# Attention scores of two query tiles made together, half-height low-key products, loads spread behind transposing DMAs, and half of a share added by VectorE

## The chip, the cores and the metric

One core of a Trainium2 chip (trn2). The time is the device time of one execution in microseconds, from the first to the last work of the core. Engines: PE (TensorE: matmul; PEld is its weight load), DVE (VectorE), ACT (ScalarE), POOL (GpSimd), SP (SyncE, which here only issues DMAs). "Tile" below is a query tile of 128 rows.

## What is computed

The reference is a layer of attention with gating experts, followed by a recurrent layer with its own experts. The change touches the attention alone. There, for 4 batches of 1024 rows of 128 and 16 heads of 64:

```python
scores = jnp.einsum('bhqd,bhkd->bhqk', q, k) * SCALE
kb = -p * jnp.log1p(a * dist)                  # dist = |key position - query position|
attn = jax.nn.softmax(scores + kb[None], axis=-1)
out = jnp.einsum('bhqk,bhkd->bhqd', attn, v)
out = out.transpose(0, 2, 1, 3).reshape(Bb, Ss, H * D)
return out @ out_w.T
```

## The kernel before

`project` makes queries, keys and values and writes each as two bf16 parts, a high one and the low remainder, to DRAM. `attend` then runs over 32 pairs of heads and batches (`it`; head pair `g` outside, batch `b` inside). One `it` has two heads `s` = 0 and 1 of eight query tiles each, so 16 tiles `n`, and 512 in all. For each tile:

- PE (`scores`, L943 to L953) makes 128 x 1024 scores in one of two PSUM buffers `score_ps`. Each half of 512 keys takes two matmuls over 128 rows: the stack of high and low queries by high keys twice (`QS` by `KS`, L951), and by low keys twice (`QS` by `KL`, L952). It waits until the tile two before has been read (`biased`) and, on a head's first tile, for the head's loads (`qk_in`).
- DVE (`bias_max`, L1018 to L1029) adds the bias table `TB` to the scores, writes them to SBUF and takes the maximum: L1028, the custom operation. It signals `biased`.
- ACT (`exp`, L1102) makes the probabilities and their sums, with four buffers `PR`.
- PE (`turn`, L960) transposes the high parts of the probabilities. DVE (L1050, odd tiles) or ACT (L1109, even tiles) copies them to `PT`.
- POOL (`low`, L1134) subtracts the high part and leaves the low one in one of four buffers `LQ`. SP (`lo_turn`, L911) transposes that with a DMA to `LO`. A buffer is free for POOL when its DMA has landed.

For each head of eight tiles there follow: PE (`by_v`) multiplies the transposed high parts by the values in four steps (L979) and the low parts in two steps of column halves (L984), 64 output rows for one half of the tiles beside 64 for the other. DVE and ACT (`take_out`) split the result into bf16 parts (L1055, L1058, L1114). PE (`out`, L997 to L999) multiplies by the head's rows of the output weights, in two PSUM buffers `pv_ps` of four tiles each. DVE (`scale_share`, L1068) scales both by the inverse sums (`SH`), and POOL (`add_share`, L1142) adds each to the accumulator `SACC`.

All engines walk through steps `u` of their own program in order, `n = u + 2` being the tile whose values step is next. In step `u` PE makes the scores of tile `u + 13`, transposes tile `u + 11`, then does the output (`n % 8 == 7`) and one values step (`n % 8 < 6`). DVE does `take_out` (`n % 8 == 6`), then tile `u + 13`, then `invert` (5), `scale_share` (7) and the copy of tile `u + 11`. ACT does its part of `take_out`, then exp of tile `u + 12`, then its copy. POOL subtracts tile `u + 11` and adds shares at `u % 8` of 6 and 7. There is no planner: the order is that of these programs, with semaphores between them.

SP's queue is in order as well. `units` (L913 to L927) issues one `lo_turn` a tile. Behind tile 2 of each head stands `load_v`. Behind tile 8 stand the six loads of the next `it`'s head 0 (`load_scores_in`, L802 to L811, 128 KB each), behind tile 15 those of its head 1. In the last batch of a head pair each is followed by `load_table` (L814 to L817): the bias table of the next pair, 128 rows of 1920 f32, 960 KB.

Of the kernel before, what the change touches and what calls it, by code (L numbers as in the profile page):

```python
# [20 lines left out]
P = 128  # L21
# [598 lines left out]
def project(nc, K, io, sb, ps, sem):  # L620
# [71 lines left out]
    with nc.Block() as block:  # L692

        @block.sync
        def _(sp):
# [16 lines left out]
            for s in range(2):  # L712
                load_scores_in(sp, K, 0, s)
                load_table(sp, K, 0, s)
# [87 lines left out]
def load_scores_in(sp, K, ix, s):  # L802

    q = K.qkscr[bass.ds(ix % B * G + ix // B, 1)].rearrange("o p k c -> (o p) k c")
    rows = slice(s * DH, s * DH + DH)
    sp.dma_start(K.QS[s][0:DH, :], q[rows, 0, :]).then_inc(K.qk_in[s], DMA)
    sp.dma_start(K.QS[s][DH:P, :], q[rows, 1, :]).then_inc(K.qk_in[s], DMA)
    sp.dma_start(K.KS[s][0:DH, :], q[rows, 2, :]).then_inc(K.qk_in[s], DMA)
    sp.dma_start(K.KS[s][DH:P, :], q[rows, 2, :]).then_inc(K.qk_in[s], DMA)
    sp.dma_start(K.KL[s][0:DH, :], q[rows, 3, :]).then_inc(K.qk_in[s], DMA)  # L810
    sp.dma_start(K.KL[s][DH:P, :], q[rows, 3, :]).then_inc(K.qk_in[s], DMA)  # L811


def load_table(sp, K, g, s):  # L814

    tab = bass.AP(tensor=K.fscr.tensor, offset=(g * 2 + s) * FLEN, ap=[[1, P], [1, TAB]])
    sp.dma_start(K.TB[s][:], tab).then_inc(K.tab_in[s], DMA)  # L817


def attend(nc, K, io, sb, ps, sem):  # L820
# [18 lines left out]
    QS, KS, KL, TB = K.QS, K.KS, K.KL, K.TB  # L839
# [12 lines left out]
    SH = [sb(f"share{i}", [P, 4, D]) for i in range(2)]  # L852
# [36 lines left out]
    def at(it, n, add):  # L889

        return it * n + add

    with nc.Block() as block:

        @block.sync
        def _(sp):
# [15 lines left out]

            def units(g, b, last=False):  # L913
                it = g * B + b
                for n in range(U):
# [5 lines left out]
                    if n in (BT, U - 1) and not (last and b == B - 1):  # L921
                        s = n // (U - 1)
                        sp.wait_ge(s_ready, at(it, U, BT * (s + 1)))
                        sp.wait_ge(biased, at(it, U, BT * (s + 1)))
                        load_scores_in(sp, K, it + 1, s)
                        if b == B - 1:
                            load_table(sp, K, g + 1, s)  # L927
# [13 lines left out]
        def _(pe):  # L941
            def scores(it, n):
                s, t, k = n // BT % 2, n % BT, n // U  # L943
                if t == 0:
                    pe.wait_ge(qk_in[s], at(it, 6 * DMA, 6 * DMA * (k + 1)))
                if not (isinstance(it, int) and it == 0 and n < 2):
                    pe.wait_ge(biased, at(it, U, n - 1))
# [748 lines left out]
```

## Time and profile before

| | us |
|---|---|
| median of 3 runs | 2019.54 |
| lowest, highest | 2015.58, 2019.97 |
| the profiled execution, its own time | 2019.78 |
| span of that execution (first to last instruction) | 2018.0 |
| mean granted clock of PE, as a share of 2.4 GHz | 0.956 |

The page begins so. Section 1 is busy time, share of the span and instructions of each engine. Section 2 cuts the span into 40 slices of 50.5 us; a digit is the busy share in tenths, PEclk the clock granted to PE, DMA the mean busy share of 16 DMA engines.

```profile
PE 1810.2 (90%) x12166; PEld 1052.0 (52%) x12356; DVE 1517.4 (75%) x2940; ACT 1149.4 (57%) x1691; POOL 1470.0 (73%) x865
...
PE   3959879999779999999999989999999999599978
...
DVE  8303548999888888878878888878888888698841
ACT  3413533222267777777777767777777777322123
POOL 4260274555579999989989899899899899655521
PEclk8779979999989999999999999999999999799989
DMA  4212483446569888888888888888888888500001
```

The attention is slices 12 to 34: the long stretch in which PE and POOL stand at 9, ACT at 7 and DMA at 8. A busy PE counts matmuls whose ends are modelled, so a 9 there is not proof that PE is the limit.

### The profile page before, as it was taken

What the parts mean: (1) busy time and instruction counts of PE and PEld (TensorE: products, weight loads), DVE (VectorE), ACT (ScalarE), POOL (GpSimd) and SP (SyncE); (2) the same over time, 40 slices, a digit from 0 to 9 for tenths busy, and PEclk for the clock granted to TensorE, in tenths of its full rate; (3) what the DMA queues carried; (4) which work ended last, traced back from release to release, by engine and by line L of the source; (5) the groups of instructions that cost most, each with busy time, mean ns of one, the idle gap of its engine ahead of it and who ended that gap; (6) DMA issues with size and microseconds to landing.
All of it is one profiled execution on the core that took longest, in us unless ns stands there. A gap on an engine that the chain in (4) does not pass through costs nothing. (4 is left out here: it accounts for less than half of the span.)

```text
span 2018.0 us, 39811 instructions
## 1 busy us (share of the span) xinstructions
PE 1810.2 (90%) x12166; PEld 1052.0 (52%) x12356; DVE 1517.4 (75%) x2940; ACT 1149.4 (57%) x1691; POOL 1470.0 (73%) x865
## 2 busy tenths in 40 slices
PE   3959879999779999999999989999999999599978
PEld 2636523333245555555555555555555555356656
DVE  8303548999888888878878888878888888698841
ACT  3413533222267777777777767777777777322123
POOL 4260274555579999989989899899899899655521
PEclk8779979999989999999999999999999999799989
DMA  4212483446569888888888888888888888500001
GB/s 138 94 42 62 127 203 128 151 146 210 167 135 180 185 194 178 193 185 180 193 180 183 186 177 184 188 182 182 187 183 184 197 184 184 135 1 1 1 6 37
DMA packets 714150, 295.28 MB, mean 146 GB/s; under 512 B 619264, under 2 KB 678658, under 8 KB 714064
## 3 DMA queue, kind: packets, MB, share of 16 engines
q1 hardware_dynamic: 678240, 257.81, 56.5%
q10 hardware_dynamic: 33792, 33.56, 4.9%
q0 software_dynamic: 2048, 3.15, 1.2%
q8 instruction: 23, 0.38, 0.1%
q14 instruction: 47, 0.39, 0.1%
HBM read 102.39 MB, written 58.85 MB: 80 GB/s over the span
## 5 line engine op out<-in xcount | busy, mean ns | idle before, releaser
L1134 POOL TENSOR_TENSOR probs_lo<-probs 128x1024 bf16<-128x1024 f32 x512 | 957.1, 1901 | 78.9 <-DMA probs_t_lo<-probs_lo 51.3
L1102 ACT ACTIVATE probs<-scores,neg_max 128x1024 f32<-128x1024 f32 x512 | 588.6, 1150 | 264.0 <-DVE neg_max L1028 232.6
L1028 DVE CUSTOM_DVE_ANT_0 scores<-score_ps,bias_tab 128x1024 f32<-128x1024 f32 x512 | 624.8, 1221 | 116.9 <-issue 111.6
L952 PE MATMUL score_ps<-k_lo_lo,q_hi_lo 128*128 128x512 bf16 x1024 | 392.8, 384 | 35.8 <-DVE ident_bf L1088 15.6
L960 PEld LDWEIGHTS turn_ps<-ident_bf,probs 128*128 128x128 bf16 x4096 | 273.2, 98 | 144.6 <-issue 25.3
L960 PE MATMUL turn_ps<-ident_bf,probs 128*128 128x128 bf16 x4096 | 314.9, 220 | 18.9 <-ACT probs L1102 18.8
L951 PE MATMUL score_ps<-k_hi_hi,q_hi_lo 128*128 128x512 bf16 x834 | 321.4, 385 | 2.1 <-DMA k_lo_lo<-qk_parts 2.1
L979 PE MATMUL pv_ps<-probs_t_hi,v_hi_lo 128*128 128x512 bf16 x1024 | 262.9, 380 | 10.4 <-DVE share L1068 7.0
L1109 ACT COPY probs_t_hi<-turn_ps 128x1024 bf16<-128x1024 bf16 x256 | 255.9, 1000 | 21.2 <-PE turn_ps L960 17.3
L798 PE MATMUL proj_ps<-xn_t,wqk 128*128 128x512 f32 x512 | 231.1, 604 | 7.2 <-DVE rotated L670 5.8
L684 POOL TENSOR_TENSOR qk_parts<-rotated,qk_parts 128x1024 bf16<-128x1024 f32 x64 | 136.3, 2132 | 111.0 <-ACT qk_parts L678 110.8
L951 PEld LDWEIGHTS score_ps<-k_hi_hi,q_hi_lo 128*128 128x128 bf16 x1024 | 100.8, 98 | 168.8 <-DVE neg_max L1028 44.5
L1050 DVE COPY probs_t_hi<-turn_ps 128x1024 bf16<-128x1024 bf16 x256 | 175.6, 686 | 0.0
L1142 POOL TENSOR_TENSOR s<-s,share 128x512 f32 (+1 forms) x128 | 163.7, 1279 | 6.9 <-DVE share L1068 6.9
L798 PEld LDWEIGHTS proj_ps<-xn_t,wqk 128*128 128x128 f32 x512 | 92.1, 189 | 146.3 <-issue 92.3
L678 ACT CAST qk_parts<-rotated 128x1024 bf16<-128x1024 f32 x64 | 66.9, 1046 | 170.6 <-DVE rotated L670 161.7
L952 PEld LDWEIGHTS score_ps<-k_lo_lo,q_hi_lo 128*128 128x128 bf16 x1024 | 101.2, 99 | 92.0 <-issue 3.0
L1350 POOL TENSOR_TENSOR q_state<-state,q_t 128x1024 f32<-128x1024 f32 x32 | 76.5, 2391 | 81.8 <-DVE state L1294 72.5
L984 PE MATMUL pv_ps<-probs_t_lo,v_hi_lo 128*64 128x512 bf16 x1024 | 134.7, 385 | 0.0
L979 PEld LDWEIGHTS pv_ps<-probs_t_hi,v_hi_lo 128*128 128x128 bf16 x1024 | 87.4, 98 | 81.1 <-DVE share L1068 19.5
L1102 ACT ACTIVATION_READ_ACCUMULATOR probs<-scores,neg_max 128x1 f32 x512 | 96.1, 188 | 0.0
L997 PE MATMUL pv_ps<-wo_parts,out_t_hi 128*128 (+1 forms) x512 | 92.7, 224 | 2.8 <-DVE out_t_lo L1058 2.8
(213 smaller groups left out, 2392.6 us busy)
## 6 DMA issues: line engine op xcount, KB each, us to landing
qk_parts<-qk_parts ACTq DMA_DIRECT2D x64, 512.0 KB, 3.2
q_hi_lo<-qk_parts SPq DMA_DIRECT2D x128, 128.0 KB, 2.8
k_hi_hi<-qk_parts SPq DMA_DIRECT2D x128, 128.0 KB, 2.9
k_lo_lo<-qk_parts SPq DMA_DIRECT2D x128, 128.0 KB, 3.0
v_hi_lo<-v_parts SPq DMA_DIRECT2D x64, 256.0 KB, 3.2
bias_tab<-bias_by_distance SPq DMA_DIRECT2D x16, 960.0 KB, 6.2
v_parts<-v_parts SPq DMA_DIRECT2D x24, 512.0 KB
probs_t_lo<-probs_lo SPq DMA_TRANSPOSE x512, 3.3
```

The lines of the kernel that those rows point to most:

```text
L684: g.tensor_tensor(parts[s][:, 1::2, :], rq[s][:], parts[s][:, 0::2, :], ALU.subtract).then_inc(lo_ready, 1)
L798: mm = pe.matmul(pp[s][:, i, :], wqk[r][:, i, :], rows, start=True, stop=True)
L951: pe.matmul(o[:, cs[c]], QS[s][:, q], KS[s][:, cs[c]], start=True, stop=False)
L952: mm = pe.matmul(o[:, cs[c]], QS[s][:, q], KL[s][:, cs[c]], start=False, stop=True)
L960: mm = pe.transpose(tp[n % 2][:, k, :], PRB[n % NP][:, k * P:k * P + P], ident16[:])
L979: mm = pe.matmul(ov[i][:], VV[h][:, k, :], PT[:, r:r + 4, k, :], start=(k == 0), stop=False, skip_group_check=True)
L1028: v.tensor_tensor_reduce(SB[n % 2][:], sp_[n % 2][:], TB[s][:, j:j + S], -1.0, 3.0e38, ALU.add, ALU.min, neg_max[:, n % 16:n % 16 + 1]).th ...
L1050: v.tensor_copy(PT[:, n % U, :, :], tp[n % 2][:]).then_inc(hi_dve, 1)
L1102: act.activation(PR[n % NP][:], SB[n % 2][:], ACT.Exp, bias=neg_max[:, m:m + 1], scale=-1.0, accum_out=row_sum[:, m:m + 1]).then_inc(exped, 1)
L1109: act.copy(PT[:, n % U, :, :], tp[n % 2][:]).then_inc(hi_act, 1)
L1134: g.tensor_tensor(LQ[n % NL][:], PR[n % NP][:], PRB[n % NP], ALU.subtract).then_inc(low_made, 1)
L1142: g.tensor_tensor(acc, acc, SH[c][:], ALU.add).then_inc(added, 1)
```

## The change

- Scores: on even tiles PE makes the scores of tiles `n` and `n + 1` in one go: the high-key products of `n`, then of `n + 1`, then the low-key products of `n` (signal), then of `n + 1` (signal).
- Low-key products: each half of 512 keys is one matmul over 64 rows instead of 128, high queries by low keys; the product of low queries by low keys is left out. The first half of the keys uses rows 0 to 63 (`QS`), the second rows 64 to 127, where a new tile `QX` holds the high queries again. `KL` holds only the half of the keys that its rows need.
- Loads: seven instead of six for each head, of 64 rows; the two of `KL` are 64 KB each, the others 128 KB. They are issued one behind each transposing DMA, behind tiles 6 to 11 for head 0 of the next `it` and 14, 15 and 0 to 3 for head 1, the last two together. The wait for `s_ready` comes ahead of the first. The bias table is loaded in four quarters of 480 columns, behind the last four of these.
- Share: DVE adds the first four tiles of each head into `SACC` itself, scaling and adding in one operation of 128 x 128 for each (four `scalar_tensor_tensor`); POOL adds the other four. One buffer `SH` instead of two.

```diff
@@ -710,8 +710,9 @@
             for s in range(4):
                 sp.wait_ge(qk_wr[s], DMA * NJ // 4 + 1)
             for s in range(2):
-                load_scores_in(sp, K, 0, s)
-                load_table(sp, K, 0, s)
+                load_scores_in(sp, K, 0, s, slice(0, 7))
+                for k in range(4):
+                    load_table(sp, K, 0, s, k)
         @block.gpsimd
         def _(g):
@@ -799,22 +800,26 @@
                         mm.then_inc(qk_ready, 1)
 
-def load_scores_in(sp, K, ix, s):
+def scores_parts(K):
+
+    low, high, every = slice(0, DH), slice(DH, P), slice(0, S)
+    return [(K.QS, low, 0, every), (K.QS, high, 1, every), (K.KS, low, 2, every), (K.KS, high, 2, every),
+            (K.QX, high, 0, every), (K.KL, low, 3, slice(0, CH)), (K.KL, high, 3, slice(CH, S))]
+
+
+def load_scores_in(sp, K, ix, s, parts):
     q = K.qkscr[bass.ds(ix % B * G + ix // B, 1)].rearrange("o p k c -> (o p) k c")
     rows = slice(s * DH, s * DH + DH)
-    sp.dma_start(K.QS[s][0:DH, :], q[rows, 0, :]).then_inc(K.qk_in[s], DMA)
-    sp.dma_start(K.QS[s][DH:P, :], q[rows, 1, :]).then_inc(K.qk_in[s], DMA)
-    sp.dma_start(K.KS[s][0:DH, :], q[rows, 2, :]).then_inc(K.qk_in[s], DMA)
-    sp.dma_start(K.KS[s][DH:P, :], q[rows, 2, :]).then_inc(K.qk_in[s], DMA)
-    sp.dma_start(K.KL[s][0:DH, :], q[rows, 3, :]).then_inc(K.qk_in[s], DMA)
-    sp.dma_start(K.KL[s][DH:P, :], q[rows, 3, :]).then_inc(K.qk_in[s], DMA)
-
-
-def load_table(sp, K, g, s):
-
-    tab = bass.AP(tensor=K.fscr.tensor, offset=(g * 2 + s) * FLEN, ap=[[1, P], [1, TAB]])
-    sp.dma_start(K.TB[s][:], tab).then_inc(K.tab_in[s], DMA)
+    for dst, to, kind, cols in scores_parts(K)[parts]:
+        sp.dma_start(dst[s][to, cols], q[rows, kind, cols]).then_inc(K.qk_in[s], DMA)
+
+
+def load_table(sp, K, g, s, k):
+
+    n = TAB // 4
+    tab = bass.AP(tensor=K.fscr.tensor, offset=(g * 2 + s) * FLEN + k * n, ap=[[1, P], [1, n]])
+    sp.dma_start(K.TB[s][:, k * n:k * n + n], tab).then_inc(K.tab_in[s], DMA)
 
 def attend(nc, K, io, sb, ps, sem):
...
@@ -910,6 +915,21 @@
                 sp.sem_inc(add_begun, 1)
                 sp.dma_start(LO[:, r, :, :], LQ[n % NL][:], transpose=True).then_inc(lo_in[n % NL], DMA)
+            def ahead(g, b, n, last):
+
+                it, s = g * B + b, (0 if 6 <= n < 12 else 1)
+                i = (n - 6) % BT
+                if i >= 6 or (n < 6 and isinstance(it, int) and it == 0) or (n >= 6 and last and b == B - 1):
+                    return
+                ix, due = (it, 0) if n < 6 else (it + 1, BT * (s + 1))
+                if i == 0:
+                    sp.wait_ge(s_ready, at(it, U, due))
+                load_scores_in(sp, K, ix, s, slice(i, i + 1 if i < 5 else 7))
+                if i >= 2 and b == (0 if n < 6 else B - 1):
+                    if i == 2:
+                        sp.wait_ge(biased, at(it, U, due))
+                    load_table(sp, K, g if n < 6 else g + 1, s, i - 2)
+
             def units(g, b, last=False):
                 it = g * B + b
                 for n in range(U):
@@ -918,13 +938,7 @@
                     if n % BT == 2 and not (isinstance(it, int) and it == 0):
                         sp.wait_ge(op_ready, at(it, 4, 2 * (s + 1) - 4))
                         load_v(it, s)
-                    if n in (BT, U - 1) and not (last and b == B - 1):
-                        s = n // (U - 1)
-                        sp.wait_ge(s_ready, at(it, U, BT * (s + 1)))
-                        sp.wait_ge(biased, at(it, U, BT * (s + 1)))
-                        load_scores_in(sp, K, it + 1, s)
-                        if b == B - 1:
-                            load_table(sp, K, g + 1, s)
+                    ahead(g, b, n, last)
             for s in range(2):
                 load_v(0, s)
@@ -940,17 +954,21 @@
         @block.tensor
         def _(pe):
             def scores(it, n):
-                s, t, k = n // BT % 2, n % BT, n // U
-                if t == 0:
-                    pe.wait_ge(qk_in[s], at(it, 6 * DMA, 6 * DMA * (k + 1)))
-                if not (isinstance(it, int) and it == 0 and n < 2):
-                    pe.wait_ge(biased, at(it, U, n - 1))
-                o, q = sp_[n % 2], slice(t * P, t * P + P)
+                s, k = n // BT % 2, n // U
+                if n % BT == 0:
+                    pe.wait_ge(qk_in[s], at(it, 7 * DMA, 7 * DMA * (k + 1)))
                 cs = [slice(c * CH, c * CH + CH) for c in range(2)]
-                for c in range(2):
-                    pe.matmul(o[:, cs[c]], QS[s][:, q], KS[s][:, cs[c]], start=True, stop=False)
-                    mm = pe.matmul(o[:, cs[c]], QS[s][:, q], KL[s][:, cs[c]], start=False, stop=True)
-                mm.then_inc(s_ready, 1)
+                pair = [(i, sp_[i], slice((n + i) % BT * P, (n + i) % BT * P + P)) for i in range(2)]
+                for i, o, q in pair:
+                    if not (isinstance(it, int) and it == 0 and n < 2):
+                        pe.wait_ge(biased, at(it, U, n + i - 1))
+                    for c in range(2):
+                        pe.matmul(o[:, cs[c]], QS[s][:, q], KS[s][:, cs[c]], start=True, stop=False)
+                for i, o, q in pair:
+                    for c in range(2):
+                        rows = slice(c * DH, c * DH + DH)
+                        mm = pe.matmul(o[:, cs[c]], (QS, QX)[c][s][rows, q], KL[s][rows, cs[c]], start=False, stop=True)
+                    mm.then_inc(s_ready, 1)
             def turn(it, n):
                 pe.wait_ge(exped, at(it, U, n + 1))
@@ -1001,7 +1019,7 @@
             def step(it, u, there):
                 n = u + LV
-                if there(u + LS):
+                if there(u + LS) and (u + LS) % 2 == 0:
                     scores(it, u + LS)
                 if there(u + LT):
                     turn(it, u + LT)
...
@@ -1062,11 +1080,18 @@
                 h = hh % 2
                 v.wait_ge(recip, at(it, 2, hh + 1))
-                for c in range(2):
-                    v.wait_ge(op_ready, at(it, 4, 2 * hh + c + 1))
-                    v.wait_ge(added, at(it, 4, 2 * hh + c + 1))
-                    v.tensor_tensor(SH[c][:], ov[c][:], last_axis(inv[:, BT * h + 4 * c:BT * h + 4 * c + 4], D),
-                                    ALU.mult).then_inc(scaled, 1)
+                v.wait_ge(scaled, at(it, 4, 2 * hh + 2))
+                v.wait_ge(op_ready, at(it, 4, 2 * hh + 1))
+                for k in range(4):
+                    row = (it % B) * BT + k
+                    acc = K.SACC[:, row, :] if isinstance(row, int) else K.SACC[:, bass.ds(row, 1), :].rearrange("p o d -> p (o d)")
+                    ins = v.scalar_tensor_tensor(out=acc, in0=ov[0][:, k, :], scalar=inv[:, BT * h + k:BT * h + k + 1],
+                                                 in1=acc, op0=ALU.mult, op1=ALU.add)
+                ins.then_inc(scaled, 1)
+                v.wait_ge(op_ready, at(it, 4, 2 * hh + 2))
+                v.wait_ge(added, at(it, 2, hh + 1))
+                v.tensor_tensor(SH[:], ov[1][:], last_axis(inv[:, BT * h + 4:BT * h + 8], D),
+                                ALU.mult).then_inc(scaled, 1)
             def step(it, u, there):
                 n = u + LV
@@ -1133,23 +1158,22 @@
                     g.wait_ge(lo_in[n % NL], at(it, DMA * U // NL, DMA * (n // NL)))
                 g.tensor_tensor(LQ[n % NL][:], PR[n % NP][:], PRB[n % NP], ALU.subtract).then_inc(low_made, 1)
-            def add_share(it, h, c):
-
-                g.wait_ge(scaled, at(it, 4, 2 * h + c + 3))
+            def add_share(it, h):
+
+                g.wait_ge(scaled, at(it, 4, 2 * h + 4))
                 g.sem_inc(add_begun, 1)
-                row = (it % B) * BT + 4 * c
+                row = (it % B) * BT + 4
                 acc = K.SACC[:, row:row + 4, :] if isinstance(row, int) else K.SACC[:, bass.ds(row, 4), :]
-                g.tensor_tensor(acc, acc, SH[c][:], ALU.add).then_inc(added, 1)
+                g.tensor_tensor(acc, acc, SH[:], ALU.add).then_inc(added, 1)
             def step(it, u, there):
                 if there(u + LT):
                     low(it, u + LT)
-                for c in range(2):
-                    if there(u) and u % BT == BT - 2 + c:
-                        add_share(it, u // BT, c)
+                if there(u) and u % BT == BT - 1:
+                    add_share(it, u // BT)
             g.wait_ge(zeroed, 1)
-            g.nop().then_inc(added, 2)
+            g.nop().then_inc(added, 1)
             run(g, step)
 
...
```

## Rows read from the trace of the kernel before

**Rows 1.** Windows, one head without a table load: busy us of each engine (x instructions).
```profile
core 0: us, PE busy (x) PEld busy (x) DVE busy (x) ACT busy (x) POOL busy (x), PEclk, DMA share, GB/s
1048.30:1065.50 17.20, 16.85 (x145) 9.99 (x148) 14.56 (x33) 13.16 (x20) 17.20 (x11) 1.00 0.84 174
```

**Rows 2.** Timeline of POOL: start, us, engine, line, operation, [idle before <- until what].
```profile
1015.35 11.15 POOL L1134 TENSOR_TENSOR probs_lo<-probs 128x1024 bf16<-128x1024 f32 x6 [5.21 <-DMA probs_t_lo<-probs_lo]
1026.46 1.27 POOL L1142 TENSOR_TENSOR s<-s,share 128x512 f32 x1
1027.69 1.90 POOL L1134 TENSOR_TENSOR probs_lo<-probs 128x1024 bf16<-128x1024 f32 x1
...
1043.74 1.29 POOL L1142 TENSOR_TENSOR s<-s,share 128x512 f32 x1
```

**Rows 3.** Instructions of L1134 and L911, ns min/median/max, first and last start, engine's waits.
```profile
L1134 POOL TENSOR_TENSOR probs_lo<-probs x512: 1887/1897/2875, 561.7 to 1730.1; 128x1024 bf16<-128x1024 f32 x171
  DMA probs_t_lo<-probs_lo: 51.3, 14
...
L911 SPq DMA_TRANSPOSE probs_t_lo<-probs_lo x512: 1230/1240/5216, 563.7 to 1732.1; - x171
```

**Rows 4.** Timeline of SP's queue: a table load; then a head's loads and transposes.
```profile
1006.21 0.42 SPq L817 DMA_DIRECT2D bias_tab<-bias_by_distance  x1
...
1060.90 0.53 SPq L806 DMA_DIRECT2D q_hi_lo<-qk_parts  x1
...
1064.89 2.69 SPq L911 DMA_TRANSPOSE probs_t_lo<-probs_lo  x2
```

**Rows 5.** The page's DMA issues: KB each, median us from issue to landing.
```profile
k_lo_lo<-qk_parts SPq DMA_DIRECT2D x128, 128.0 KB, 3.0
v_hi_lo<-v_parts SPq DMA_DIRECT2D x64, 256.0 KB, 3.2
```

**Rows 6.** Timeline of all engines, parts of two tiles.
```profile
1002.74 0.61 PE L960 MATMUL turn_ps<-ident_bf,probs 128*128 128x128 bf16 x8
...
1003.18 1.03 PE L979 MATMUL pv_ps<-probs_t_hi,v_hi_lo 128*128 128x512 bf16 x4
...
1009.26 0.61 PE L960 MATMUL turn_ps<-ident_bf,probs 128*128 128x128 bf16 x8
...
1009.80 1.05 PE L984 MATMUL pv_ps<-probs_t_lo,v_hi_lo 128*64 128x512 bf16 x8
1010.61 0.08 DVE L1028 DVE_READ_ACCUMULATOR2_ANT neg_max<- 128x1 f32 x1
...
1010.78 0.10 PEld L951 LDWEIGHTS score_ps<-k_hi_hi,q_hi_lo 128*128 128x128 bf16 x1 [0.41 <-DVE neg_max L1028]
...
1011.87 1.22 DVE L1028 CUSTOM_DVE_ANT_0 scores<-score_ps,bias_tab 128x1024 f32<-128x1024 f32 x1 [0.57 <-issue]
```

**Rows 7.** Timeline of DVE at a head's first tiles and at its scaling.
```profile
1200.33 1.22 DVE L1028 CUSTOM_DVE_ANT_0 scores<-score_ps,bias_tab 128x1024 f32<-128x1024 f32 x1 [0.57 <-issue]
...
1203.59 1.22 DVE L1028 CUSTOM_DVE_ANT_0 scores<-score_ps,bias_tab 128x1024 f32<-128x1024 f32 x1
...
1206.49 1.28 DVE L1068 TENSOR_TENSOR share<-pv_ps,inv_sum 128x512 f32<-128x512 f32 x2
```

**Rows 8.** Groups of DVE by shape: count | busy us, mean ns | idle before.
```profile
L250 DVE SCALAR_TENSOR_TENSOR s<-s,ln_moe_rstd,attn_nb_rows 128x128 f32<-128x128 f32 x32 | 8.8, 347 | 0.1
```

**Rows 9.** Timelines of ACT and of POOL, an exp and its subtraction.
```profile
963.02 1.15 ACT L1102 ACTIVATE probs<-scores,neg_max 128x1024 f32<-128x1024 f32 x1 [1.43 <-DVE neg_max L1028]
...
964.17 0.99 ACT L1109 COPY probs_t_hi<-turn_ps 128x1024 bf16<-128x1024 bf16 x1
...
964.34 1.90 POOL L1134 TENSOR_TENSOR probs_lo<-probs 128x1024 bf16<-128x1024 f32 x1 [0.34 <-ACT probs L1102]
```

**Rows 10.** Timeline of PE after a long stop, and the window that follows.
```profile
1167.30 1.03 PE L960 MATMUL turn_ps<-ident_bf,probs 128*128 128x128 bf16 x8 [4.33 <-ACT probs L1102]
...
1166.53:1169.94 3.41, 2.64 (x25) 2.65 (x26) 1.56 (x4) 2.85 (x6) 3.41 (x3) 0.50 1.08 222
```

More of the change, by code:

```diff
@@ L837, in attend @@
     recip = sem("recip")
-    QS, KS, KL, TB = K.QS, K.KS, K.KL, K.TB
+    QS, QX, KS, KL, TB = K.QS, K.QX, K.KS, K.KL, K.TB
     VV = [sb(f"v_hi_lo{s}", [P, BT, 2 * DH], BF16) for s in range(2)]
@@ L851, in attend @@
     OL = [sb(f"out_t_lo{i}", [P, CH], BF16) for i in range(2)]
-    SH = [sb(f"share{i}", [P, 4, D]) for i in range(2)]
+    SH = sb("share", [P, 4, D])
     ot_hi, wo_ready = [sem(f"ot_hi{c}") for c in range(2)], sem("wo_ready")
@@ L1022, in bias_max @@
                 if t == 0:
-                    v.wait_ge(tab_in[s], (it + n // U) // B * DMA + DMA)
+                    v.wait_ge(tab_in[s], (it + n // U) // B * (4 * DMA) + 4 * DMA)
                 if not (isinstance(it, int) and it == 0 and n < 2):
@@ L1615, in program @@
             K.QS = [sb_in(f"q_hi_lo{s}", [P, S], BF16) for s in range(2)]
+            K.QX = [sb_in(f"q_hi_again{s}", [P, S], BF16) for s in range(2)]
             K.KS = [sb_in(f"k_hi_hi{s}", [P, S], BF16) for s in range(2)]
```

## The prediction, made before the changed kernel was built or run

> **What bounds the kernel now.** The windows of the attention stage come first. In a head without a table load [rows 1] POOL is busy for the whole 17.2 us and PE for 16.85; DVE and ACT have slack. A head is eight query tiles, so POOL's timeline [rows 2] is next: eight subtractions (L1134) and two share additions (L1142) repeat every 17.28 us (1026.46 to 1043.74) without idle. The stage, from the first L1134 to the last, is 1730.1 + 1.9 - 561.7 = 1170.3 us [rows 3] for 64 heads: 64 x 17.28 = 1105.9, plus 51.3 in which POOL waited for transposing DMAs [rows 3], plus 13.1 of filling and small waits. One of the waits for DMA is the 5.21 us in [rows 2]; the table load of 960 KB stands just before it in SP's queue (1006.21 in [rows 4]). There are 14 such loads, two in each of seven changes of head pair. The profiled execution took 2019.8 us (the median of the runs is 2019.5), so all else is 2019.8 - 1170.3 = 849.5 us, which the change doesn't touch but for the first loads.
>
> **What the parts save by themselves.** POOL loses one of two additions, 1.23 us (1026.46 to 1027.69 in [rows 2]): 16.05 a head. SP issues eight transposes, six loads and one load of values in a head. Two transposes in a row took 2.69, one issue is 1.24 [rows 3], so they stand 1.45 apart; the six loads before them took 1064.89 - 60.90 = 3.99, or 0.66 each [rows 4]. A load moved behind a transpose costs the same 0.66, for it is an instruction with its own registers wherever it stands. With seven loads and the values SP needs 8 x 1.45 + 8 x 0.66 = 16.9 us, and 4 x 0.6 more in the 14 heads with table quarters. On PE a 128-column transpose passes in 0.056 (eight in 0.45), a 512-column product of L979 in 0.217 (four in 0.87), and a column half of L984 in 0.096, two side by side [rows 6]. Row halves aren't in these rows. I take them to run side by side like the column halves, the nearest row: the four low-key products of a tile pair then take 0.43 where they took 0.87. The other bound is one after another, nothing saved. DVE gives one multiplication of 0.6 (the second of two in [rows 7]) for four of 128x128. The nearest row, L250, has 0.347 each [rows 8]; quarters of 0.6 would be 0.15. I take 0.25 each, 1.0 for four, as they don't wait for one another. If those savings were all, SP would be last with 16.9.
>
> **What the new order adds: the tile pair.** So far the scores of tile n+1 are made while VectorE reads tile n; two PSUM buffers allow it. In the pair, s_ready of the even tile n comes only after the first products of n+1, and these go into the buffer that tile n-1 leaves when it is biased. So when DVE has done n-1, tile n can't be ready. The price of that: DVE ends an L1028 at 1010.61 + 0.08 = 1010.69 and PE's weight load follows at 1010.78, 0.09 later; four matmuls start from 1010.78 on, the last at 1011.43, and L1028 starts at 1011.87, 0.44 later [rows 6]. New: 0.09 + 2 x 0.217 + 0.44 = 0.96, and a change of array shape.
> The column halves price that change: a block of transposes starts 0.44 before L979 (1002.74 to 1003.18) but 0.54 before L984 (1009.26 to 1009.80), and eight halves that need some 0.86 held the array for 0.98 [rows 6]. So 0.1 in and 0.1 out, and the same for row halves, nearest to them in kind: 0.2 a pair on PE, 0.1 in DVE's gap, which becomes 1.06.
> The Trainium skill says in "TensorEngine Tiling (Array Packing)", Key Properties, that changing the tiling mode drains TensorE, which speaks against a pair that changes it twice; the 0.1 above agrees. Without a price for it the period below is 0.3 us shorter, the time 19 us less.
>
> **One head worked through.** Zero is the start of L1028 on the head's first tile, 16. In us:
> - Tile 17's L1028 starts at 3.26, behind the reciprocal and three operations on the output (1200.33 to 1203.59 in [rows 7]), and ends at 4.49.
> - With the gap, tile 18 runs from 5.55 to 6.78. ACT must first copy tile 16's transposes (PE 5.63 to 6.08, copy 6.25 to 7.25 by the 0.99 of [rows 9]), so exp(18) starts at 7.25. POOL starts 1.32 after an exp does (963.02 to 964.34 in [rows 9]): low(18) from 8.55 to 10.4, the share addition to 11.65, low(19) to 13.5.
> - DVE scales after tile 18: op_ready is there at 6.9, four small operations end at 7.95, the multiplication at 8.6; tile 19 from 8.6 to 9.83.
> - PE: first products of 21 at 9.92. A pair with two value steps costs PE 4 x 0.217 + 0.43 + 0.2 + 2 x 0.45 + 2 x 0.87 = 4.13; the pair with a column-half step 4.33. (DVE would need 2 x 1.23 + 1.06 = 3.5.) So first products of 25 start at 18.4, and tile 24's L1028 at 18.4 + 0.43 + 0.1 + 0.44 = 19.4.
> DVE and PE now alternate where they overlapped, and need 19.4 us a head, though neither is busy for more than 17.
> **And the late loads.** All six loads of a half used to follow tile 8 (or 15). Now the last two stand behind the transpose of tile 11 (or 19), and scores(16) (or 24) wait for both. In my head that transpose is issued at 13.55, its loads at 15.0 and 15.65, and the last lands 3.0 later, at 18.65 (k_lo_lo in [rows 5]; 64 KB instead of 128 saves little, since 256 KB take only 3.2). First products of 24 start at 18.75, not at 17.95, and those of 25 at 19.2: tile 24's L1028 at 20.15. So 20.1 a head. A table quarter issued behind them at 16.3 lands by 19.5 (the row of 256 KB) and costs nothing. The moved waits on s_ready and biased cost nothing either: they ask for tiles that PE made well before POOL's subtraction of the tile whose transpose stands in front; transposes are queued behind them, and these are later by their own low part.
> The bursts that held the transposes are gone, and with them the 51.3 us.
>
> **The sum.** 64 x 20.1 = 1286.4, plus 13.1, plus 849.5 is 2149; for the first two heads, whose loads are there, 1 less: 2148 us, 6.4% slower. Bounds: row halves one after another, 0.6 a head more (2186); a landing 0.3 earlier or later, 19 us less or more; small DVE operations of 0.15 or 0.35, nothing as long as the loads come last; no price for the change of shape, 19 less. Together 2110 to 2200.
>
> **Rivals.**
> - The parts save what they save and the rest overlaps: SP's 16.9 is the period. 64 x 16.9 = 1081.6, tables 14 x 2.4 = 33.6, with 13.1 and 849.5 1978, faster by 2.1%. For it: PE gets shorter, and four buffers lie between exp and the transposes. Against: no buffer lies between the two score tiles and DVE, and buffers behind can't help a front that comes late. It decides once a pair's gap on DVE is under 0.5 us.
> - The pair costs less than I sum, and the loads come in time: no price for shapes, small operations cheap, 18.5 a head: 64 x 18.5 + 862.6 = 2047. For it: in my head the loads are late by only 0.75, little for a chain of ten steps.
> - In between, 18.0 to 18.2 a head: no difference, because the 51.3 us pay for the pair.
> - The clock falls. After 4.33 us without a matmul eight transposes took 1.03 instead of 0.61, and the granted clock of the next 3.41 us was 0.50, 1.2 GHz [rows 6, 10]. In my head PE is idle for 2.1 us before tile 19's products and has work for four fifths of the time; no row shows what that does. One such stretch a head costs up to half of 3.41, 1.7 us: 64 x 1.7 = 109, 2257.
>
> **How the numbers follow.** Forecast 0.57; pair alone 0.18; falling clock 0.07; SP's period 0.13; no difference 0.05. The range runs from the no-difference case (2015) to past the forecast's own upper bound (2215), and leaves out SP's period and the falling clock, 0.20. A measurement of this kernel can tell 0.2% (4 us) from no change. Faster by more than that 0.13, within it 0.05, slower by more 0.82.
>
> **What would show it.** In the trace of after: POOL's L1134 waits for ACT every head, and heads are 20 us long; on DVE some 2.3 us from an odd tile's L1028 to the even one's after it, 1.23 inside a pair; PE waits for k_lo_lo at each head's first scores; the low-key products start two at a time; no stop of POOL at the table loads. It would be wrong if POOL or SP had no idle time, or if an even tile's L1028 followed the odd one's without a gap.

## The result, and the profile after

| | us |
|---|---|
| before, median | 2017.56 |
| changed, median of 4 runs | 2190.10 (2184.83 to 2198.07) |
| ratio | 1.0835 (95%: 1.0806 to 1.0863) |
| the profiled execution of the changed kernel | 2198.07, span 2196.3 |
| its mean granted clock | 0.937 of 2.4 GHz |

The changed kernel is 8.35% slower by the ratio on record (the two medians divided give 8.55%, within its interval of 8.06 to 8.63); 6.4% was forecast. "Before" is the same kernel as above, with one more run beside the changed one. Two sections of its page, the busy times and three lines of the 40 slices (54.9 us each):

```profile
PE 1823.5 (83%) x12198; PEld 977.1 (44%) x12356; DVE 1551.2 (71%) x3132; ACT 1148.4 (52%) x1691; POOL 1404.5 (64%) x801
...
PE   3959689998688888888788888788888888779978
...
POOL 4340555555687777777687787777777777654521
PEclk8879789999799999999999999999999999988989
```

In slices 11 to 34 PE has gone from 9 to 8 and POOL from 9 to 7. POOL does less (1470.0 us became 1404.5) in more time: it isn't the limit. The instructions of its subtraction (line 1134 before, 1159 now) say what it waits for:

```profile
L1159 POOL TENSOR_TENSOR probs_lo<-probs x512: 1886/1895/3938, 562.1 to 1902.0; 128x1024 bf16<-128x1024 f32 x171
its engine sat idle before it (us, times) until:
  ACT probs L1127: 311.6, 325
  DMA probs_t_lo<-probs_lo: 2.2, 3
```

Against [rows 3]: the 51.3 us of waits for transposing DMAs have gone to 2.2, as the change intends, and 311.6 us of waits for exp have come. The stage lasts 1902.0 + 1.9 - 562.1 = 1341.8 us where it took 1170.3. That is the whole loss, but for 7 us: all else took 856.3, against 849.5.

**The head that was worked through.** DVE in one head without a table load and without a fall of the clock; its first tile starts at 1189.71, line 1046 is the former 1028:

```profile
1189.71 1.22 DVE L1046 CUSTOM_DVE_ANT_0 scores<-score_ps,bias_tab 128x1024 f32<-128x1024 f32 x1
...
1192.99 1.22 DVE L1046 CUSTOM_DVE_ANT_0 scores<-score_ps,bias_tab 128x1024 f32<-128x1024 f32 x1
1194.13 0.69 DVE L1068 COPY probs_t_hi<-turn_ps 128x1024 bf16<-128x1024 bf16 x1
1195.25 1.22 DVE L1046 CUSTOM_DVE_ANT_0 scores<-score_ps,bias_tab 128x1024 f32<-128x1024 f32 x1 [0.43 <-issue]
1196.87 1.13 DVE L1088 SCALAR_TENSOR_TENSOR s<-pv_ps,inv_sum,s 128x128 f32 x4 [0.39 <-PE pv_ps L1017]
1197.91 0.68 DVE L1093 TENSOR_TENSOR share<-pv_ps,inv_sum 128x512 f32<-128x512 f32 x1
1198.52 1.22 DVE L1046 CUSTOM_DVE_ANT_0 scores<-score_ps,bias_tab 128x1024 f32<-128x1024 f32 x1
1199.66 0.69 DVE L1068 COPY probs_t_hi<-turn_ps 128x1024 bf16<-128x1024 bf16 x1
1200.78 1.22 DVE L1046 CUSTOM_DVE_ANT_0 scores<-score_ps,bias_tab 128x1024 f32<-128x1024 f32 x1 [0.43 <-issue]
1201.93 1.22 DVE L1046 CUSTOM_DVE_ANT_0 scores<-score_ps,bias_tab 128x1024 f32<-128x1024 f32 x1
```

| start of L1046, us from the head's first | tile 17 | 18 | 19 | 20 | 24 |
|---|---|---|---|---|---|
| forecast | 3.26 | 5.55 | 8.6 | 10.9 | 20.1 |
| measured | 3.28 | 5.54 | 8.81 | 11.07 | 19.77 |

(Tile 20's forecast is the 9.83 at which tile 19 ends plus 1.06; the next head starts at 1209.48.) Before each even tile DVE is idle, its copy hiding part of the gap: 0.43 of 1.12. Inside a pair tiles stand 1.15 apart. The window of the whole head says what this means. In [rows 1], before, PE was busy for 16.85 of 17.2 us and POOL for all of them; now:

```profile
core 0: us, PE busy (x) PEld busy (x) DVE busy (x) ACT busy (x) POOL busy (x), PEclk, DMA share, GB/s
1189.71:1209.49 19.78, 16.54 (x149) 8.55 (x149) 15.69 (x38) 13.91 (x21) 15.64 (x9) 1.00 0.72 153
```

No engine is full. PE and DVE hand each other the two score buffers in turn.

The end of this head shows the loads too:

```profile
1204.82 1.14 SPq L815 DMA_DIRECT2D k_lo_lo<-qk_parts  x2
...
1208.31 0.81 PE L966 MATMUL score_ps<-k_hi_hi,q_hi_lo 128*128 128x512 bf16 x3 [0.39 <-DMA k_lo_lo<-qk_parts]
```

The last loads are issued 15.11 us after the head's start and PE goes on at 18.60; 15.0 and 18.75 were worked out. But PE came there at 18.21 instead of 17.95, so it waited 0.39 and not 0.8: the pair took longer than worked out, the loads cost less.

**The array.** PE's timeline at one tile pair: the last high-key product, the four half-height ones (the two that run together have their own names, `QS` and `QX`), then the transposes:

```profile
1049.82 0.38 PE L966 MATMUL score_ps<-k_hi_hi,q_hi_lo 128*128 128x512 bf16 x1
...
1050.13 0.39 PE L970 MATMUL score_ps<-k_lo_lo,q_hi_lo 64*128 64x512 bf16 x1
1050.13 0.39 PE L970 MATMUL score_ps<-k_lo_lo,q_hi_again 64*128 64x512 bf16 x1
...
1050.36 0.38 PE L970 MATMUL score_ps<-k_lo_lo,q_hi_lo 64*128 64x512 bf16 x1
...
1050.67 0.62 PE L978 MATMUL turn_ps<-ident_bf,probs 128*128 128x128 bf16 x8
```

Row halves start together, as taken from the column halves. Steps inside a shape are 0.22, steps into and out of the half-height shape 0.31: 0.1 each way, as charged. The prediction cites from the Trainium skill, "TensorEngine Tiling (Array Packing)", Key Properties, that a change of tiling mode drains TensorE. The trace agrees in so far as each change costs 0.1 us; what happens inside the array it doesn't show.

### The profile page after: what moved, and what is told of

It is laid out like the page before. It is cut to its first block and busy times, and to the rows that moved or that the text cites. A ratio compares the mean times of both kernels' runs of the same rounds, so it can differ in the third digit from the quotient of the medians.

```text
span 2196.3 us, 40193 instructions
## 1 busy us (share of the span) xinstructions
PE 1823.5 (83%) x12198; PEld 977.1 (44%) x12356; DVE 1551.2 (71%) x3132; ACT 1148.4 (52%) x1691; POOL 1404.5 (64%) x801
## 5 line engine op out<-in xcount | busy, mean ns | idle before, releaser
L1159 POOL TENSOR_TENSOR probs_lo<-probs 128x1024 bf16<-128x1024 f32 x512 | 966.8, 1899 | 313.9 <-ACT probs L1127 311.6
L1046 DVE CUSTOM_DVE_ANT_0 scores<-score_ps,bias_tab 128x1024 f32<-128x1024 f32 x512 | 616.1, 1220 | 158.8 <-ACT probs L1127 77.7
L966 PE MATMUL score_ps<-k_hi_hi,q_hi_lo 128*128 128x512 bf16 x866 | 261.4, 394 | 220.7 <-DVE neg_max L1046 156.7
L1134 ACT COPY probs_t_hi<-turn_ps 128x1024 bf16<-128x1024 bf16 x256 | 259.1, 1012 | 258.0 <-PE turn_ps L978 257.8
L978 PEld LDWEIGHTS turn_ps<-ident_bf,probs 128*128 128x128 bf16 x4096 | 254.6, 101 | 177.0 <-issue 142.9
L978 PE MATMUL turn_ps<-ident_bf,probs 128*128 128x128 bf16 x4096 | 329.5, 226 | 0.5 <-ACT probs L1127 0.5
L966 PEld LDWEIGHTS score_ps<-k_hi_hi,q_hi_lo 128*128 128x128 bf16 x1024 | 82.3, 98 | 362.4 <-DVE neg_max L1046 235.8
L970 PE MATMUL score_ps<-k_lo_lo,q_hi_again 64*128 64x512 bf16 x512 | 165.3, 405 | 0.0
L970 PE MATMUL score_ps<-k_lo_lo,q_hi_lo 64*128 64x512 bf16 x512 | 165.3, 405 | 0.0
L678 ACT CAST qk_parts<-rotated 128x1024 bf16<-128x1024 f32 x64 | 66.9, 1046 | 170.6 <-DVE rotated L670 162.0
L1045 DVE MEMSET wait_holder<- 128x1 f32 x512 | 30.2, 59 | 117.1 <-PE score_ps L970 114.8
L1015 PE MATMUL pv_ps<-wo_parts,out_t_hi 128*128 (+1 forms) x512 | 102.9, 238 | 2.7 <-DVE out_t_lo L1076 2.7
L1016 PE MATMUL pv_ps<-wo_parts,out_t_hi 128*128 (+1 forms) x512 | 101.9, 236 | 0.0
```

The lines of the kernel that those rows point to most:

```text
L966: pe.matmul(o[:, cs[c]], QS[s][:, q], KS[s][:, cs[c]], start=True, stop=False)
L970: mm = pe.matmul(o[:, cs[c]], (QS, QX)[c][s][rows, q], KL[s][rows, cs[c]], start=False, stop=True)
L978: mm = pe.transpose(tp[n % 2][:, k, :], PRB[n % NP][:, k * P:k * P + P], ident16[:])
L1046: v.tensor_tensor_reduce(SB[n % 2][:], sp_[n % 2][:], TB[s][:, j:j + S], -1.0, 3.0e38, ALU.add, ALU.min, neg_max[:, n % 16:n % 16 + 1]).th ...
L1134: act.copy(PT[:, n % U, :, :], tp[n % 2][:]).then_inc(hi_act, 1)
L1159: g.tensor_tensor(LQ[n % NL][:], PR[n % NP][:], PRB[n % NP], ALU.subtract).then_inc(low_made, 1)
```

## The experiments

The chips that ran them differ: the kernel before took 1992.8 to 2019.8 us on them. So each kernel is given as its ratio to runs of the kernel before on the same chip, and a total in us that was expected before a run is to be read against 2018 us. Head lengths are distances between the starts of L1028 (its line in each kernel) on first tiles. Two groups of heads are told apart: the 21 "at the tables" (the last two of each head pair and the first of the next, at seven changes) and the 40 others, without the very first two. Even and odd heads (the first and second of an `it`) differ too: 17.5 and 18.1 us in the kernel before.

| kernel | ratio | 95% |
|---|---|---|
| changed, again | 1.0847 | 1.0814 to 1.0879 |
| a_early: loads two tiles earlier | 1.0688 | 1.0660 to 1.0715 |
| a_single: no pair | 1.0395 | 1.0367 to 1.0423 |
| a_single_early: both | 1.0060 | 1.0039 to 1.0081 |
| a_filler: PE kept busy | 1.0771 | 1.0746 to 1.0796 |
| b_pair: before, pair alone | 1.0671 | 1.0639 to 1.0702 |
| b_spread: before, loads alone | 1.0594 | 1.0561 to 1.0626 |
| b_share: before, share alone | 1.0062 | 1.0042 to 1.0082 |
| b_half: before, half height alone | 0.9999 | 0.9985 to 1.0014 |
| b_quarters: before, table quarters alone | 1.0155 | 1.0129 to 1.0180 |
| b_quarters_early | 0.9917 | 0.9893 to 0.9941 |
| b_spread_early | 0.9925 | 0.9909 to 0.9942 |

**The changed kernel again**, to stand beside its variants.

> The changed kernel itself once more, so that it stands on the same chip as its variants. Ratio to the kernel before 1.08 again. By both theories the difference to the variants is what counts; heads without a clock fall and without table loads 20.1 us.

Measured: 1.0847. Heads without a fall of the clock and away from the tables took 20.09 us.

**Loads two tiles earlier.**

```diff
-                it, s = g * B + b, (0 if 6 <= n < 12 else 1)
-                i = (n - 6) % BT
+                it, s = g * B + b, (0 if 4 <= n < 10 else 1)
+                i = (n - 4) % BT
...
```

> The changed kernel with its loads two tiles earlier (behind tiles 4 to 9 and 12 to 15, 0, 1). Theory (the last loads come late by the 37.6 us that PE waits for k_lo_lo in the trace of the change): those waits go, heads without a clock fall take about 19.4 us instead of 20.2, total about 2145 (2135 to 2155). Rival (the alternation of PE and DVE in the tile pair is all there is, a wait for a load only takes the place of one for DVE): no change, 2190. If the lateness were the whole loss: 1980.

Measured: 1.0688, that is 1.6% or 32 us less than the changed kernel, and just above the range (1.058 to 1.068 in ratios). PE no longer waits for loads. Nearly all even heads took 19.55 us, close to the 19.4 worked out for PE and DVE alone; the odd ones took 21.4, and those are the ones with a stretch of 3.41 us at 1.2 GHz in them. Two heads in a row (columns as in the window above; the granted clock is the third number from the end):

```profile
895.62:915.16 19.54, 16.53 (x149) 8.55 (x149) 15.68 (x37) 13.91 (x21) 15.94 (x10) 1.00 0.78 163
915.16:936.58 21.42, 18.76 (x156) 9.60 (x157) 15.76 (x39) 13.91 (x21) 16.56 (x10) 0.92 0.73 150
```

Where the gain lies matters more than its size. The 21 heads at the tables fell from 21.83 us in the changed kernel's first profile (21.59 in its second) to 20.20, which is 29 to 34 us, all of it. The 40 others took 20.60 (20.49) and take 20.61 now: those without a fall of the clock are shorter, the even ones 19.55 instead of 19.9, but 23 of the 40 have a fall where 15 had. And with the loads early the heads at the tables are no longer than the rest, though the quarters are still there. So lateness was real, above all at the tables, and elsewhere its gain went to the clock.

**Tile by tile.**

```diff
-                if there(u + LS) and (u + LS) % 2 == 0:
+                if there(u + LS):
                     scores(it, u + LS)
...
```

and `scores` makes one tile: two high-key products, two half-height ones.

> The changed kernel with the scores made tile by tile as before (each tile's high-key products, then its two half-height ones), loads where the change puts them. Theory (two chains of about the same length: the pair, and the way from the transpose of tile 19 over its loads to tile 24 and on to tile 27's transpose, which is 5.1 + 1.2 + 13 = 19.3 us without a pair): the gap on DVE goes but the heads stay at 19 to 19.5 us, total 2105 to 2140. Rival (costs add; without the pair only SP's queue and the 0.6 us of late loads are left, some 17.6 a head): 1990 to 2010.

Measured: 1.0395, below what the theory gave (in ratios 1.043 to 1.06) and well above the additive rival. Heads away from the tables (and without a fall) took 18.75 us, not 19.3; with the loads early as well they take 18.2 (the next run), so the second chain is real but 0.5 shorter than summed. PE waited for k_lo_lo 61 times, 74.6 us, twice the 37.6 us of the changed kernel: without the pair, PE comes sooner to the late loads. Two thirds of the wait, 49.6 us, are at the tables.

**Both.**

> Both at once: tile by tile, and loads two tiles earlier. Theory of two chains: only now is neither in the way, and a head falls to what SP (16.9) or PE needs (8 tiles of 0.65 + 0.2 for scores, 3.6 for transposes, 5.6 for values, 1.3 for output: 17.4): 17.4 to 17.8 a head, 1980 to 2010, so more gained than by the two apart together. Rival (additive): the sum of the other two runs' gains.

Measured: 1.0060. Apart, the two gain 0.0452 and 0.0159 (from 1.0847), 0.061 together; both at once gain 0.079. Each mechanism hides part of the other, as two chains of nearly one length do; part of the surplus is the clock, at 1.2 GHz within the heads for 115 us in a_early, 43 in a_single and 28 here. The length itself was missed: 17.4 to 17.8 a head was expected (ratio 0.981 to 0.996), and two heads take 36.39 us, 18.2 each. b_share, below, has 36.48, so what is left is about the price of the moved share.

**PE kept busy.**

```diff
+                    for again in range(4 if i == 0 and n % BT == 2 else 0):
+                        for c in range(2):
+                            pe.matmul(o[:, cs[c]], QS[s][:, q], KS[s][:, cs[c]], start=True, stop=True)
```

> The changed kernel with eight more high-key matmuls (1.7 us, overwritten by the real ones) before the tile pair of each head in which PE stands idle for some 2 us. They put nothing on the path. Theory (the granted clock falls because PE is idle there, and the 29 heads with a fall are 1.3 us longer for it): few or no stretches at 1.2 GHz in the attention, about 35 us less, 2155. Rival (the falls only hit times in which PE isn't last; the longer heads are the ones with table quarters): 2190 with the falls gone.

Measured: 1.0771, 0.0076 or 15 us less than the changed kernel, with eight matmuls more a head. The time at 1.2 GHz within the heads fell from 92 us (the changed kernel again) to 29. The fall is a real cost. 15 us is half of what I expected, but a third of the time at 1.2 GHz is still there: of 25 heads with a fall 11 are left. Away from the tables, even heads without a fall took 19.8 us with the added matmuls and without, odd ones 20.3 and 20.2, so the matmuls cost little or nothing themselves.

**The pair alone.** From the kernel before, with full-height products and its loads and shares:

```diff
+                for i, o, q in pair:
+                    if not (isinstance(it, int) and it == 0 and n < 2):
+                        pe.wait_ge(biased, at(it, U, n + i - 1))
+                    for c in range(2):
+                        pe.matmul(o[:, cs[c]], QS[s][:, q], KS[s][:, cs[c]], start=True, stop=False)
+                for i, o, q in pair:
+                    for c in range(2):
+                        mm = pe.matmul(o[:, cs[c]], QS[s][:, q], KL[s][:, cs[c]], start=False, stop=True)
+                    mm.then_inc(s_ready, 1)
...
```

> The kernel before with the tile pair alone (full-height products, loads and shares as before). Theory (PE and DVE alternate): DVE's gap is 0.09 + 0.43 + 0.22 + 0.44 = 1.2 us a pair, PE needs 8 x 0.217 + 0.9 + 1.74 = 4.4 us for a pair with two value steps, and a head takes 19.5 to 19.9 us: ratio 1.05 to 1.07. Rival (the pair is harmless, the late loads and shape changes make the loss): ratio 1.00 to 1.01.

Measured: 1.0671, at the upper end. DVE's idle time shows before an even tile (the numbers in brackets are idle time alone; its copy fills the rest of the gap):

```profile
1115.12 1.22 DVE L1031 CUSTOM_DVE_ANT_0 scores<-score_ps,bias_tab 128x1024 f32<-128x1024 f32 x1
...
1117.49 1.22 DVE L1031 CUSTOM_DVE_ANT_0 scores<-score_ps,bias_tab 128x1024 f32<-128x1024 f32 x1 [0.54 <-issue]
1118.64 1.22 DVE L1031 CUSTOM_DVE_ANT_0 scores<-score_ps,bias_tab 128x1024 f32<-128x1024 f32 x1
```

Tiles inside a pair start 1.15 apart, so 1117.49 - 1115.12 - 1.15 = 1.22 is the gap; 1.2 was worked out. Two heads took 40.35 us, where the kernel before takes 35.6. That is 20.2 a head and more than the 19.5 to 19.9 worked out: the gap is right, the sum of PE's part too short.

This run also prices a fall of the clock. All even heads took 19.88 us and all odd ones 20.47, but for the twelve with a fall, which took 1.5 to 1.6 more. Two even heads with the same instructions, the first with a granted clock of 0.92, the second with 1.00:

```profile
797.72:819.17 21.45, 19.08 (x152) 10.63 (x151) 15.33 (x34) 13.90 (x21) 17.15 (x11) 0.92 0.66 142
839.64:859.52 19.88, 17.51 (x152) 10.01 (x151) 15.32 (x34) 13.90 (x21) 17.15 (x11) 1.00 0.71 154
```

And the heads at the tables are no longer than others here, with the large loads as before: the pair's slack on POOL takes up the stops.

**The loads alone.** Six loads, one behind each transpose, table quarters behind the last four; all else as before.

> The kernel before with the loads alone moved (six of 128 KB, one behind each transpose of tiles 6 to 11 and 14 to 3, table quarters behind the last four). Theory (the last load lands too late for the next head): 18.6 to 19 us a head in place of 17.8, and longer at the tables: ratio 1.03 to 1.05, with PE waiting for k_lo_lo. Rival (what the move is for: the 51 us of stops at the tables go and nothing comes instead): ratio 0.975.

Measured: 1.0594, more than expected. Heads away from the tables and without a fall took 19.6 us. The instructions that wait are those of each head's first scores:

```profile
L965 PE MATMUL score_ps<-k_hi_hi,q_hi_lo x1024: 379/379/634, 554.1 to 1850.0; 128*128 128x512 bf16 x171
...
  DMA k_lo_lo<-qk_parts: 130.2, 62
```

62 of 62 heads that can wait do, 2.1 us on average. SP's transposes mostly start only when DVE is three to four tiles further (counted in the trace of before at tiles 11 and 3), so a load behind the transpose of tile 11 is issued as DVE is at tile 14 or 15. Here PE waits 130.2 us in all and in a_single 74.6; POOL's second addition, which is still there and would make the queue later, may be the reason, but no run shows it.

**The share alone.**

> The kernel before with the share alone moved: DVE adds the first four tiles of each head. Theory: POOL falls to 16.1 us a head, but PE needs some 17.1 and the table stops stay, so little is gained: ratio 0.985 to 1.0. Rival (POOL was the limit and DVE has room): 1.2 us a head, ratio 0.965. Third (DVE's 1.15 + 0.6 for a head's scaling delays the next tile's scores and costs as much as it gives): 1.00 to 1.01.

Measured: 1.0062, the third case. POOL has 1.23 us less a head, and two heads take 36.48 us instead of 35.60. 0.44 a head is also what DVE's scaling is longer: four operations at 0.26 and one of 0.6, for two of 0.6. DVE's path passes on all that is added to it, so it had no slack, and POOL, though busy all the time in [rows 1], didn't set the length of a head.

**Half height alone.** Tile by tile, seven loads in one burst.

> The kernel before with the half-height low-key products alone, tile by tile, and seven loads in one burst. Theory (a change of array shape costs PE 0.1 us in and 0.1 out, so a tile's scores take 0.43 + 0.1 + 0.22 + 0.1 = 0.85 against 0.87): no gain, ratio 0.998 to 1.004. Rival (the halving is worth its 0.22 us a tile, at least in the tiles in which PE sets the step of 2.17 us): 1.95 a step and ratio 0.97 to 0.98.

Measured: 0.9999. By itself this could also mean that PE doesn't set the length. The timeline shows that PE gets hardly shorter in any case:

```profile
999.86 0.59 PE L950 MATMUL score_ps<-k_hi_hi,q_hi_lo 128*128 128x512 bf16 x2
1000.38 0.39 PE L953 MATMUL score_ps<-k_lo_lo,q_hi_lo 64*128 64x512 bf16 x1
...
1000.71 0.62 PE L961 MATMUL turn_ps<-ident_bf,probs 128*128 128x128 bf16 x8
```

A tile's scores take 0.85 us (999.86 to 1000.71) where four full-height products take 0.87: the halving saves 0.22 us, and the two changes of shape cost 0.2.

**Table quarters alone**, behind tiles 9 to 12 and 0 to 3.

> The kernel before with the bias table alone in quarters, one behind each transpose of tiles 9 to 12 (first head) and 0 to 3 (second), the six score loads staying where they were. Theory (of all parts of the change this one meets a stop that is real, and it brings nothing late, since the quarters have four or more tiles until they are needed): POOL's waits for transposing DMAs and most clock falls go, 30 to 50 us less, ratio 0.975 to 0.985. Rival (SP's queue, full by then, only shifts the stop to the following tiles): ratio 0.995 to 1.0.

Measured: 1.0155; both were wrong. POOL's waits for transposing DMAs fell to 14.2 us, and the first tile of a new head pair waits in their place. SP's queue and DVE:

```profile
825.33 0.43 SPq L819 DMA_DIRECT2D bias_tab<-bias_by_distance  x1
...
829.10 1.22 DVE L1032 CUSTOM_DVE_ANT_0 scores<-score_ps,bias_tab 128x1024 f32<-128x1024 f32 x1 [6.87 <-issue]
```

The last quarter is issued when DVE has long done tile 15 (L1032 started at 820.41); DVE goes on 3.77 us after the issue, when it has landed.

**Quarters earlier, and everything earlier.** The same quarters behind tiles 5 to 8, 13 to 15 and 0; and b_spread with its first load behind tile 3 instead of 6.

> As b_quarters, with the quarters three to four tiles earlier: behind tiles 5 to 8 for the first head, 13 to 15 and 0 for the second. In b_quarters DVE stood 6.9 us at the first tile of a new head pair, because SP's transposes run three to four tiles behind DVE and the last quarter stood behind tile 12. Theory: now they land in time and the stops of POOL stay away: ratio 0.975 to 0.985. Rival (whatever is put in place of the one large load costs the same or more on SP's queue or in the DMA engines): 1.00 to 1.015.

> As b_spread (six loads and the quarters, one behind each transpose), everything three tiles earlier: behind tiles 3 to 8 and 11 to 15 and 0. Theory (the 6% of b_spread are lateness and nothing else): PE's waits for k_lo_lo go and the ratio is 0.97 to 0.985, like b_quarters_early, since spreading or bursting six loads is the same for a queue with slack. Rival (spreading costs by itself, as each load delays each transpose): 1.01 to 1.03.

Measured: 0.9917 and 0.9925. Both have the sign of the theory, not its size. POOL still waits for transposing DMAs for 34.1 and 36.0 us, two thirds of the 51.3; the longest stop is 4.3 and 3.6 us instead of 5.4, and most falls of the clock are gone (13 and 17 us at 1.2 GHz within the heads, 30 before). Nor was there as much to gain as 51.3: against heads of 17.53 and 18.07, those of the kernel before are 29.5 us longer in all, and of these 12 and 15 are left. Between b_spread and b_spread_early lie three tiles of lead and 6.7%. These two are the only kernels here that beat the one before, by 0.8%.

## Why the prediction was right, and where it wasn't

**The tile pair** was right as a mechanism: alone it costs 6.7%, and its gap was 1.2 as worked out. The head of the changed kernel followed the working within 0.4 us.

**The late loads** were right as a mechanism; their size was not. 0.7 us a head was forecast, for every head. PE waited for k_lo_lo in 38 heads, and of the 37.6 us only 9.4 lie in the 40 heads away from the tables. a_early gained 32 us, 0.5 a head if spread evenly, but all of it at the tables. That heads away from the tables and without a fall took 20.12 us, and 20.1 was forecast, is luck in part, since two terms were off in opposite ways. The pair alone is some 19.7 (an estimate: even heads of a_early take 19.55, odd ones 21.41 less the 1.53 of a fall in b_pair) where 19.4 was summed, and the late loads add the other 0.4. b_pair too was longer than summed. That both chains are of about one length, which made the sum of the parts (1.067 + 1.059) larger than the whole, was in the working.

**Half height, change of shape, small operations** were as taken: side by side, 0.1 each way, 0.26 each (0.25 taken).

**What bounds the kernel now** was read wrongly. I took POOL's 17.28 us, from a head in which it never waited, as the length of all heads. That head follows a stop of 5.21 us [rows 2], when POOL has work waiting. The starts of L1028 alternate between heads of 17.5 and 18.1, 17.8 on average, and b_share shows that POOL gives nothing. 64 x 17.8 = 1139 leaves 31 us of the stage for stops of all kinds, not 51.3 + 13.1: a good part of POOL's waits for DMAs at the tables fell into slack. This didn't spoil the forecast, as it took the whole stage's 1170.3 away and put its own sum there; only the 13.1 us called small waits, which are part of this misreading, were carried into the new sum without a ground.

**The tables** are the first term that was missed. I said that they cost nothing behind the last loads, and that the stops were gone with the bursts. In the changed kernel the heads around the seven changes of head pair take 21.24 us with the clock up and 22.28 with a fall, where the others take 20.12 and 21.30: over the 21 heads 9 x 1.12 + 12 x 0.98 = 22 us. a_early shows that this is lateness too: with the same quarters and loads two tiles earlier nothing of it is left. The working saw that the last quarter lands in time, but not what the quarters do to SP's queue. The steps of SP there:

```profile
880.51 0.43 SPq L822 DMA_DIRECT2D bias_tab<-bias_by_distance  x1
881.13 1.26 SPq L916 DMA_TRANSPOSE probs_t_lo<-probs_lo  x1
882.62 0.40 SPq L907 DMA_DIRECT2D v_hi_lo<-v_parts  x1
883.12 0.83 SPq L815 DMA_DIRECT2D q_hi_again<-qk_parts  x1
884.13 0.44 SPq L822 DMA_DIRECT2D bias_tab<-bias_by_distance  x1
884.76 1.24 SPq L916 DMA_TRANSPOSE probs_t_lo<-probs_lo  x1
...
890.40 1.89 PE L966 MATMUL score_ps<-k_hi_hi,q_hi_lo 128*128 128x512 bf16 x4 [3.44 <-DMA k_lo_lo<-qk_parts]
```

From transpose to transpose 3.6 us with all four kinds of load in between, and the last scores load lands that much later: the PE wait after this one was 3.4 us.

**The clock** is the second. It was a rival of its own, at 0.07 and as a fall in every head; it came in 28 of 62 heads and costs some 1.2 us each (20.12 to 21.30), 33 us, on top of the forecast's mechanism. It should have been a term with a share, not an alternative. b_pair has 1.5 for a fall, and with a_filler 15 us came back for 63 us less at 1.2 GHz. Together 22 + 33 = 55, less the 13 carried wrongly, is the 42 us between the stage forecast (1299.5) and the one measured (1341.8). How the 55 divides is less sure: counting the second head of a new pair in place of the last but one of the old makes it 29 and 28.

**SP's period** as a rival (1978) fell: even with neither pair nor late loads (a_single_early) two heads take 36.39 us, 18.2 each and not 16.9. **The quarters' gain**, which I took as sure in the sum, is what I had least ground for: alone they cost 1.6% where they first stood, and gain 0.8% at best.

## What to carry to other kernels

Two buffers between two engines are worth one tile of overlap; whoever makes both tiles in one go has spent it, and no buffer further on gives it back. An operation moved behind another one in a queue inherits its lag: count how many tiles that queue runs behind the engine that needs the result, before choosing the place, and move loads as early as their buffer comes free. An engine that is busy all the time in a window is not yet the limit; take work from it and see whether the period moves.

## What the hardware showed that I had not expected

A stop shorter than the 4.33 us of [rows 10] can already be followed by half a clock. In the changed kernel PE had stops of 1.84 and 2.17 us in one head and was granted half speed next, with the transposes at 0.89 for eight instead of 0.62:

```profile
1059.56 1.03 PE L966 MATMUL score_ps<-k_hi_hi,q_hi_lo 128*128 128x512 bf16 x4 [1.84 <-DMA k_lo_lo<-qk_parts]
...
1065.83 0.61 PE L966 MATMUL score_ps<-k_hi_hi,q_hi_lo 128*128 128x512 bf16 x2 [2.17 <-DVE neg_max L1046]
...
1066.90 0.89 PE L978 MATMUL turn_ps<-ident_bf,probs 128*128 128x128 bf16 x8
...
1059.56:1067.29 7.73, 5.50 (x45) 2.41 (x47) 5.54 (x13) 3.95 (x6) 3.94 (x4) 0.99 0.91 184
1067.29:1070.70 3.41, 3.41 (x36) 3.41 (x35) 2.14 (x7) 2.15 (x3) 2.32 (x2) 0.53 0.33 64
```

Heads with the same stops also went without a fall (the one from 1189.71 has 2.17 too), so one stop alone doesn't decide it. In a_early each head has one such stop of 2.17 us, and after the first two every second head has the fall; in b_pair, with the same stop, every fifth. What sets this rhythm no run here shows. And chips differ ahead of the attention: the first subtraction started at 534.0 to 535.6 us in six of these traces and at 557.4 to 562.1 in the others. In the attention no such difference shows: b_half, on a chip of the first kind, has heads of 17.5 and 18.1 us, like the kernel before on one of the second.
